# Scores in 64 by 64 parts, the adapter's up product in fp32r, router products in column halves, and new orders of steps on five engines

## The reference

```python
w_down = down_project * dg + db                  # dg, db, ug, ub: conditions @ gamma or beta, by sequence
act = relu(x @ w_down)                           # 256 -> 64
x1 = act @ (up_project * ug + ub) + x            # 64 -> 256
h = rmsnorm(x1, w1); qkv = h @ qkv_w + qkv_b     # 16 query heads, 4 key heads of 64, rope on q and k
logits = q @ k.T / 8, causal; attn = exp(logits - logaddexp(lse, sink))
x2 = x1 + (attn @ v) @ proj_w + proj_b
h2 = rmsnorm(x2, w2); glogits = h2 @ gate_w + gate_b   # 32 experts, the 4 best, softmax over the 4
y2 = sum over the 4 of weight * (silu(h2 @ Wg) * (h2 @ Wu)) @ W_down
out = x + x2 + y2
```

## Time and profile before

| | us |
|---|---|
| median of 3 runs | 1088.05 (1086.29 to 1090.01) |
| profiled execution, its own time | 1092.17 |
| its span, first to last instruction | 1090.3 |
| mean granted TensorE clock, share of full | 0.945 |
| PE busy | 957.5 |
| DVE busy | 787.7 |
| POOL busy | 552.4 |
| ACT busy | 512.5 |

### The profile page before, as it was taken

How to read it: one execution, slowest core, us unless ns; L and a number is a source line. 1 busy time by engine, 2 the same in 40 slices (tenths; PEclk the granted TensorE clock), 3 DMA queues, 4 the chain that set the end, 5 groups by cost and what they waited for, 6 DMA issues and landing times.

```text
span 1090.3 us, 19211 instructions
## 1 busy us (share of the span) xinstructions
PE 957.5 (88%) x6168; PEld 780.9 (72%) x6192; DVE 787.7 (72%) x1867; ACT 512.5 (47%) x1192; POOL 552.4 (51%) x515
## 2 busy tenths in 40 slices
PE   3869999898998989989887459999999999999985
PEld 1547676686675867758665348888888888888874
DVE  3767777776886778867564637777777777777777
ACT  0213453534535345363455236566565666666641
POOL 2424556757858578585756713333333333333340
PEclk8779999999999999999898669999999999999998
DMA  7226766678766787667785788687687867773499
GB/s 212 57 62 196 214 211 191 223 245 249 252 188 235 246 243 258 187 238 227 233 299 203 252 301 276 227 294 239 235 289 236 280 222 260 243 253 111 142 367 343
DMA packets 127674, 251.80 MB, mean 231 GB/s; under 512 B 18706, under 2 KB 66327, under 8 KB 127002
## 3 DMA queue, kind: packets, MB, share of 16 engines
q1 hardware_dynamic: 83866, 187.59, 52.5%
q0 software_dynamic: 13872, 34.64, 8.7%
q10 hardware_dynamic: 29840, 28.34, 8.5%
HBM read 136.19 MB, written 102.66 MB: 219 GB/s over the span
## 4 chain that ended last, share of the span: by engine, by line
PE 61%; DVE 15%; DMA 8%; POOL 6%; issue 5%; ACT 3%; SPq 1%; POOLq 0%; DVEq 0%; ACTq 0%
PE scores L962 10%; PE gbank L962 9%; PE gbank L832 8%; PE gbank L981 5%; PE gbank L757 5%; PE scores L981 4%; DVE ring L1369 4%; DMA rows_in<-lists 3%; PE scores L793 3%; POOL lists L670 3%; PE gbank L936 2%; PE scores L936 2%; PE scores L971 1%; PE gbank L821 1%; PE gbank L735 1%
## 5 line engine op out<-in xcount | busy, mean ns | idle before, releaser
L692 POOL DMA_INDIRECT pick_rows<-rows_out,pair_i x161 | 160.8, 999 | 269.4 <-ACT rows_out L1213 260.4
L677 POOL TENSOR_TENSOR ring<-ring 128x512 fp32r<-128x512 f32 x96 | 122.0, 1278 | 59.5 <-ACT ring L1150 56.2
L832 PE MATMUL gbank<-w_o,ring 128*128 128x256 f32 x512 | 130.4, 413 | 13.1 <-DVE ring L1352 7.5
L962 PE MATMUL scores<-ring,in_part 128*128 x486 | 135.3, 414 | 1.3 <-DVE in_part L1606 1.3
L962 PE MATMUL gbank<-ring,in_part 128*128 x480 | 131.8, 409 | 0.0
L832 PEld LDWEIGHTS gbank<-w_o,ring 128*128 128x128 f32 x512 | 104.8, 209 | 34.3 <-issue 9.9
L757 PE MATMUL gbank<-h_t,w_qk 128*128 128x512 f32 x480 | 121.7, 407 | 6.8 <-DVE h_t L1356 4.2
L670 POOL DMA_INDIRECT lists<-put_rows,slot_i x104 | 102.5, 986 | 26.6 <-issue 24.4
L1369 DVE SCALAR_TENSOR_TENSOR ring<-gbank,b_qk,rope 128x512 f32<-128x512 f32 x160 | 108.5, 743 | 5.8 <-PE gbank L757 5.6
L757 PEld LDWEIGHTS gbank<-h_t,w_qk 128*128 128x128 f32 x480 | 90.3, 193 | 29.7 <-issue 5.8
L962 PEld LDWEIGHTS scores<-ring,in_part 128*128 128x128 f32 x486 | 86.6, 192 | 16.8 <-issue 1.7
(11 more groups left out here) (194 smaller groups left out, 1886.0 us busy)
## 6 DMA issues: line engine op xcount, KB each, us to landing
w_parts<-ring SPq DMA_DIRECT2D x192, 256.0 KB
ring<-w_parts SPq DMA_DIRECT2D x32, 1536.0 KB
rows_in<-lists ACTq DMA_DIRECT2D x161, 136.0 KB
ring<-in_W_up SPq DMA_DIRECT2D x64, 256.0 KB
picks<-pick_rows SPq DMA_DIRECT2D x8, 2048.0 KB
ring<-in_W_down SPq DMA_DIRECT2D x32, 256.0 KB
q_r<-rot SPq DMA_DIRECT2D x16, 512.0 KB, 5.5
q_r<-ring SPq DMA_DIRECT2D x16, 512.0 KB
```

The lines of the kernel that those rows point to most:

```text
L677: e.tensor_tensor(lower, lower.bitcast(F32), upper.bitcast(F32), ALU.subtract).then_inc(s_lower, 1)
L692: e.indirect_dma_start(out=pick_rows, out_offset=bass.IndirectOffsetOnAxis(ap=pair_i[:, i:i + 1], axis=0), in_=rows_out[i % NY][:, :], in_ ...
L832: e.matmul(bank[:, 0:D], y_t[:, n // REP, n % REP, :, :].rearrange("p b s -> p (b s)"), w_o[:, n, :], start=n == 0, stop=False)
L962: ins = e.matmul(front[i % FRONTS], in_parts[i % IN_BUFS][x][:, c, :], ring[:, bass.ds(at + y * WE + c * 2 * DFF, 2 * DFF)], start=k == 0, ...
```

## The change

Four products or orders are changed, all in part 1.

1. `score`: each product is cut into two, with 64 stationary columns each (`h`), which go to the two column halves of the array. 32 products for a tile in place of 16.
2. `route_pick`: each product is cut likewise, into two column halves with all 128 rows: 16 products of 64 stationary by 32 moving columns in place of 8.
3. `up`: the relu's result is split into an upper fp32r part (ACT, in partitions 0 to 63) and a lower one (a new DVE step `relu`, partitions 64 to 127), the weights likewise in two matrices (at the start, ACT and DVE, in `cond`). A block takes five fp32r matmuls of 512 columns in place of three fp32 ones.
4. `ORDERS` of all five engines are new. `tag` now also waits until its buffer of rows is free, as `pack` did.

```diff
         def up(m, banks):
+            w.wait_ge(s_up_split, 1)
             w.wait_ge(s_act, m + 1)
-            for c in range(KC + 1):
+            for c in range(KC):
                 bank = take(banks[c])
-                e.matmul(bank[:, :], w_up_ones[:, c * P:(c + 1) * P], act[:, :], start=True, stop=True).then_inc(
-                    s_up, 1)
+                e.matmul(bank[:, :], w_up[:, 0, c * P:(c + 1) * P], act[:, :], start=True, stop=False)
+                e.matmul(bank[:, :], w_up[:, 1, c * P:(c + 1) * P], act[:, :], start=False, stop=True).then_inc(s_up, 1)
+            e.matmul(take(banks[KC])[:, :], ones_r[:, :], act[:, :], start=True, stop=True).then_inc(s_up, 1)
...
                 for go in range(2):
-                    ins = e.matmul(out[go][:, c, :], q_r[i][half[go], gp, a, 2 * at.start:2 * at.stop], k_r[i][half[go], gp, at],
-                                   start=False, stop=c == 7, skip_group_check=True)
+                    for h in range(2):
+                        q_at = slice(2 * at.start + h * T, 2 * at.start + (h + 1) * T)
+                        ins = e.matmul(out[go][h * T:(h + 1) * T, c, :], q_r[i][half[go], gp, a, q_at],
+                                       k_r[i][half[go], gp, at], start=False, stop=c == 7, skip_group_check=True)
...
                 for c in range(KC):
-                    ins = e.matmul(bank[:, s * E:(s + 1) * E], x2_t[:, c, (lo + s) * P:(lo + s + 1) * P], w_gate[:, c, :],
-                                   start=c == 0, stop=c == KC - 1)
+                    for h in range(2):
+                        at = (lo + s) * P + h * T
+                        ins = e.matmul(bank[h * T:(h + 1) * T, s * E:(s + 1) * E], x2_t[:, c, at:at + T], w_gate[:, c, :],
+                                       start=c == 0, stop=c == KC - 1)
...
+        def relu(m):
+            d_sum = tmp[0][2]
+            w.wait_ge(s_d_sum, m + 1)
+            w.wait_ge(s_act_upper, m + 1)
+            if m:
+                w.wait_ge(s_up, (KC + 1) * m)
+            e.scalar_tensor_tensor(out=act[CH:P, :], in0=d_sum[0:CH, :], scalar=0.0, in1=act[0:CH, :].bitcast(F32),
+                                   op0=ALU.max, op1=ALU.subtract).then_inc(s_act, 1)
...
 ORDERS = {
     "PE": ("""
-        down cond up sums pair pair pair pair pair down value score up
+        cond down up sums pair pair pair pair pair value down score up
```

More of the change, by code:

```diff
@@ L71 @@
     "PE": ("""
-        down cond up sums pair pair pair pair pair down value score up
+        cond down up sums pair pair pair pair pair value down score up
     """, """
-        value score turn_prob score sums attend route_turn project route_turn pair pair turn_prob score
-        route_turn route_turn attend route_pick value pair route_count project pair turn_prob pair
-        attend value value project turn_prob down attend score up project
+        score route_turn turn_prob score route_turn route_turn attend sums value project turn_prob
@@ L77 @@
+        pair route_turn score pair route_pick attend pair value project route_count pair pair
+        turn_prob value attend value down project turn_prob score attend up project
     """, """
-        score turn_prob value score attend route_turn route_turn project turn_prob route_turn route_turn
-        attend value route_pick project turn_prob route_count score attend value route_turn route_turn
-        project turn_prob attend route_pick route_count route_turn project route_turn route_pick
@@ L81 @@
-        route_count route_pick route_count
+        route_turn route_turn score turn_prob route_turn score attend value route_turn project
+        turn_prob route_pick value attend project route_turn route_count turn_prob route_turn score
+        attend project turn_prob value attend route_turn project route_pick route_turn route_pick
+        route_count route_pick route_count route_count
     """),
     "DVE": ("""
-        cond down up weights apply pair pair pair pair pair constants down value softmax_a softmax_b up
+        cond down relu up weights apply pair pair pair pair pair value constants down relu softmax_a
@@ L85 @@
+        up softmax_b
     """, """
-        softmax_a value softmax_b apply project softmax_a pair pair softmax_b route_pick value
-        route_count pair project route_list pair softmax_a pair value softmax_b project value down
-        softmax_a up project softmax_b
+        softmax_a softmax_a softmax_b apply value project softmax_b pair pair route_pick pair
+        softmax_a value project route_count pair pair value route_list softmax_b value down project
+        relu softmax_a up softmax_b project
@@ L146 @@
 GROUPS = len(ROOTS)
-TIMES = {"cond": 1, "weights": 1, "constants": 1, "load_middle": 1, "load_late": 1, "fill_before": NM, "down": NM, "up": NM, "sums": NM, "apply": NM, "pair": NM * NPAIR,
+TIMES = {"cond": 1, "weights": 1, "constants": 1, "load_middle": 1, "load_late": 1, "fill_before": NM, "down": NM, "relu": NM, "up": NM, "sums": NM, "apply": NM, "pair": NM * NPAIR,
          "move": NM * NPAIR, "load_x_t": NM, "root": GROUPS, "route_pick": GROUPS, "route_count": GROUPS,
@@ L1153, in scalar_program @@
             banks = banks_for.get((name, k))
-            if name == "down":
+            if name == "cond":
+                cond()
+            elif name == "down":
                 down(k)
```

88 lines of the change are left out of this document (51 added, 37 removed).

## The result

The changed kernel took 1033.84 us (median of 4 runs, 1033.34 to 1035.57) where the kernel before took 1088.36 (1086.29 to 1090.01): a ratio of 0.951 [0.948, 0.955], faster by 54.5 us. The profiled execution took 1033.4 of its own time, span 1031.5. The controls further down add a second half to the result: run again on another chip, the same kernel is not faster at all.

A forecast was written before the change was run, and what follows sets the result against it. PE, 91% busy, was taken to set part 1's pace. Steady 32.3 us (85% of 38.0) plus start 3.1 less tail 1.5 made 33.9, hence 1054 against the median of 1088.05; range 1037 to 1076.

The forecast's parts named there:

- The sizes of the steps: PE in part 1: score 2.00 to 1.14 us, route_pick 1.97 to 1.14, up 2.84 to 1.4.
- The load is the price, and not the product: PE's score and route_pick: loading 128 stationary fp32 columns sets 0.11 us a place; 64 columns should take 0.057.
- New orders could also shrink these waits; I give them nothing: PE's waits for other engines in part 1, some 6 us a period: gain from new orders counted as nothing.
- the fourth rival: Part 1: new orders let all 38 us show and take 1.5 us of idle a period, 1038; chance 0.15.
- I take 85%: Steady part of part 1: of 38.0 us of PE's time saved, 85% shows, 32.3 us.
- the first rival: Part 1: DVE takes over, periods stay near 65 us, half the steady gain goes, 1070; chance 0.12.
- The tail: End of part 1: POOL's puts and splits unchanged; two thinner covers lose 1.5 us, between 0 and 5.
- The start: Start of part 1: 1.5 us from work not behind DVE's weight scaling, 1.6 from first score; 3.1 in all.
- The third rival: Score on PE: handing over records sets the pace, 128 take 4 us; 53 us slower, 1141; chance 0.08.

The follow-up runs named there:

- e1: The kernel before with the new orders of all engines but the old score, route_pick and up, on chip 11: 1052.92 us, ratio 0.967.
- the later set: Second set on chip 11, kernel before 1087.13: the changed kernel again 1034.82 us, new orders with old steps again 1054.65 us.
- e2: The changed kernel with the old orders, new steps kept, relu right behind down on DVE, on chip 11: 1089.05 us, ratio 0.997.
- e15: The changed kernel with POOL's subtraction over 128 of 512 columns (work left out), on chip 3: 1016.63 us, ratio 0.931.
- e9: The changed kernel with nothing edited, run as a control on chip 10: 1088.66 us, ratio 0.999.
- e5: The changed kernel with POOL's subtraction over 128 of 512 columns (work left out), on chip 15: 1110.91 us.
- e8: The changed kernel with SP's four writes of fill rows a block made as one transfer, on chip 15: 1100.71 us.
- e6: The changed kernel with weight-third loads from the sixth on bringing 128 of 512 columns (work left out), on chip 15: 1076.48 us.
- e18: The changed kernel with one fill transfer a block and POOL's puts in twos and threes, on chip 0: 1072.99 us, ratio 0.984.
- e12: The changed kernel with POOL's puts in twos and threes between subtractions instead of eight in a row, on chip 11: 1045.22 us.
- e17: The changed kernel with SP's four fill writes a block as one transfer, on chip 0: 1102.29 us, ratio 1.011.
- e10: The changed kernel with one fill transfer a block and the old score of 32 records, on chip 10: 1111.45 us.

## Why the prediction was wrong

**The sizes of the steps** were right: 1.14, 1.14 and 1.4 us worked out for score, route_pick and up, 1.16, 1.12 and 1.43 measured. So was the saving of PE's time: over six periods PE is busy for 32.7 us less. "The load is the price, and not the product" fits all three.

**"New orders could also shrink these waits; I give them nothing"** is the step that failed. The orders give 37 of the 55 us (e1; 32 of 52 in the later set), by the table 30 in the six periods and 12.5 in the tail. The rows allowed a bound: 6.6 us of idle PE in 67.7, seven times, is 46 us, and e1 took 4.5 of the 6.6. I knew of the size and put only a quarter of it into the fourth rival, because the order's effect could not be read from single rows.

**"I take 85%"** failed the other way. On top of the new orders the lighter steps give 18 of 38 us, 48%; for the score alone it is 41%. In the four later periods nothing of it shows, and none with the old orders (e2). The two errors have opposite signs and hid each other in part. That the later periods came out at 62 to 63, as forecast, is luck: e1 has them at 61 to 64 with the heavy steps.

What takes PE's place there is not DVE by itself, the first rival, but POOL and what hangs on it: e15 takes 10 us from POOL in a block and gets 18 us in all. The waits of two periods of the changed kernel had pointed there, with the weights' transfers first and the pauses between POOL's puts third:

```profile
ACT ring L1167 <- DMA w_parts<-ring: 20.6, 7, 6.5
...
POOL lists L672 <- issue: 8.9, 31, 0.3
```

**The tail** was the largest miss. For the stretch from the last `sums` to part 2 the forecast comes to 2.1 us of gain: 3.6 from the four scores and the router product in it, less 1.5 of loss. Measured is 17.4, and e1 gets 12.5 of it. From the last `sums` to the router product that gates the first put, PE needed 83.3 us before and 64.9 after; it is busy there for 58.3 in place of 71.0, part of that before at the lower clock, and idle for 6.6 in place of 12.3. The new orders also put two attends less ahead of that product. The forecast moved it only by what PE saves ahead of it and took the rest as fixed.

**The start**: 3.1 forecast, 2.7 measured.

**The third rival**, "PE can't be fed", had 0.08 and a price of 1141. Something of it happens on three of five chips, in another form: not the pace of all short records, but a stall of some 7 us once or twice a block, which in e9 eats the gain and no more. My argument against it, that single records start fast, was true and beside the point: the first 40 records of a stalled score come without a gap too.

**What stays open.** Why chips 0, 10 and 15 have the stall and chips 3 and 11 not. As a control the changed kernel itself was run on 10 and 11 only, and e5's kernel on 15 and 3 (as e15); the other chips are told apart by variants. On each chip only one set was run, on chip 11 two; that it is the chip and not the hour is the simplest reading of five, not shown. Also open is what the puts hold up: PE's records come late, and so do DVE and ACT behind it. A late block of instructions is not needed for it: in e8 blocks were brought at 388.0 and 404.7, the stall ran from 395.8 to 402.6; in e9 one was brought within a stall, at 317.2, in 1.1 us. The Trainium skill (Runtime: NRT & Kernel Launch, "Instruction fetch mechanics") says that such fetching is mostly hidden; no run here contradicts that. What shorter loads (e6) and the one fill transfer (e8) do without the stall, and what the spread order alone does with it, was not measured, so how much of the loop is transfers and how much SP is open too; shown is only POOL's part. No version here that does all the work beats the changed kernel where there is no stall. On chip 0 e18 beats the kernel before by 16 us (0.984 [0.980, 0.988]); the changed kernel was not run beside it, and e12's order gives up 10 us where there is no stall.

## What to carry to other kernels

Idle time of the bounding engine is worth as much as its work: before pricing a lighter instruction, give a change of order a range of its own, up to the idle time in the period's row. Then ask which engine is next; here cutting the work of POOL, 77% busy, shortened the period, and DVE's 86% was no sign that it must be DVE. A period that comes out as forecast proves nothing until each half of the change has been run alone. A gain that depends on dense short matmuls is to be timed on more than one chip, and "issue" gaps inside a run of equal records are the sign to look for. Where one engine issues many indirect transfers in a row and this sign shows, spreading them out is worth a trial (29 us between e17 and e18), and so is its price where it does not show (10 us, e12).

## What the runs showed of the hardware

- Four quarters of the array together take fp32 products of 64 by 64 by 64 at 18 ns a record, 36 a product (64 records in 1.16 us), where the mean length of one is 227 ns.
- On chips 0, 10 and 15, PE's records fall to a few per 0.7 to 1.4 us, beginning 3.8 to 5.9 us after the first of eight indirect transfers of POOL and lasting about until they end. In the same traces DVE and ACT start late on what PE's records show as finished, by up to 6.7 us in e10 (332.3 to 338.9). On chips 3 and 11 no run shows it.
- After such a stall PE's granted clock is lower: 1.98 us for an attend of 1.09 in e9, and 0.90 to 0.92 of full over a period for 0.97.
- With POOL's subtractions cut from 512 to 128 columns some small DVE steps get quicker: a cast of 128 by 16 takes 239 ns in e15 and 739 in the changed kernel.
